# Three semaphores in turn for the indirect transfers of a routed layer, in place of two

## The chip, the cores and the metric

One Trainium2 chip, one NeuronCore of it. The metric is the device time of one execution in microseconds, as a median of several executions. PE is TensorE, DVE is VectorE, ACT is ScalarE, POOL is GpSimd, SP is SyncE.

## What is computed

A block of three layers on x of 4 x 1024 x 128 (f32): half a feed-forward layer, an attention layer, the same half feed-forward layer again, each on the layer norm of x and added to x.

```
x = x + 0.5 * ffn(layernorm(x))
x = x + attn(layernorm(x))       # 16 heads of 8, causal, with a slope bias
x = x + 0.5 * ffn(layernorm(x))

def ffn(x):                      # N = 4096 rows, D = 128, HID = 256
    gates = softmax(x @ router_w)            # 14 routed experts
    top_v, top_i = top_k(gates, 2)           # normed over the two
    routed = sum over the two chosen e: g_e * silu(rms(x)*rw_e @ W1_e) @ W2_e
    shared = sum over 2 shared experts, all rows
```

## The kernel before

The 4096 rows are 32 tiles of 128 rows, in two groups r = 0 and r = 1 of 16 tiles (GT). A feed-forward layer f (0 or 1) does its routed experts sparsely. DVE works out for each row its two experts and the place of each in a buffer `sorted_x[r]` in HBM, in which rows of one expert stand together. POOL then **scatters**: for each of the 16 tiles and each of the 2 choices one indirect transfer (L824) writes 128 rows of 512 bytes from SBUF to those places, so 32 transfers (MOVES) for a group. SP then loads `sorted_x` back in 23 pairs of tiles (L658, 128 KB each, `xld`), the first when all 32 scatters of the group have landed (L652). PE transposes a pair (L1819), multiplies it with the first weights of its experts (L1831), ACT does the silu, PE multiplies with the second weights (L1843), ACT brings the result to SBUF and stores it (`sorted_y`, L996). DVE copies the weights of the pair three ahead (L1373), each copy behind the product that frees the buffer. When all pairs of a group are stored, POOL **gathers**: 32 indirect transfers (L841) bring the rows back in order, and DVE multiplies them with the gates and adds them to x (`add_part`, L1182, eight parts for a group, each of which needs the transfers of its block of four tiles).

All 256 indirect transfers have one number n in a row, and a program order on POOL: scatter(0,0), scatter(0,1), gather(0,0), gather(0,1), then, in the second feed-forward layer, scatter(1,0), scatter(1,1), gather(1,0), gather(1,1), where the first number is f and the second r. What lies between them on POOL matters. The square roots for the attention's first norm (`norm(0)`, L745 to L747) stand behind the 18th gather of (0,0), waiting on DVE's statistics; a copy of the values (`values(0)`, L862) follows the 32nd; behind gather(0,1) POOL itself adds six of the eight parts of that group (`pool_adds`, L890 and L895), and only then does `norm(1)`, on whose result DVE waits in step 0 of the second group of heads of the first batch (`normed`, L1480; PE's next steps stand behind DVE). The other two parts of (0,1) are DVE's.

`keep_pace` holds back some scatters until PE has come to a given product, so that they don't all start at once.

A transfer waits on the semaphore that it will itself increment. These are the lines (L820 to L826 for a scatter, L839 to L844 for a gather):

```
n = MOVES * SCATTERS[GROUPS * f + r] + TOP_K * t + k
if n >= MOVE_SEMS:
    pool.wait_ge(s_moved[n % MOVE_SEMS], 16 * (n // MOVE_SEMS))
keep_pace(f, r, TOP_K * t + k)
nc.gpsimd.indirect_dma_start(...).then_inc(s_moved[n % MOVE_SEMS], 16)
```

and those who need the rows wait on all of the semaphores:

```
def moved(first, count):
    return [(s_moved[i], 16 * (sum(n % MOVE_SEMS == i for n in range(first + count))))
            for i in range(MOVE_SEMS) if any(n % MOVE_SEMS == i for n in range(first, first + count))]
```

At the end of the second feed-forward layer PE and ACT do 24 units of the shared experts (L1743, L950, L1762), 4 for each chunk of x left; gather(1,1) and its eight add_parts run beside them, four of the parts placed among the units (LATE_ADD_AT), four behind the last unit's sum (L1360). The result goes out in eight transfers (L703), each behind its block's adds.

Of the kernel before, what the change touches and what calls it, by code (L numbers as in the profile page):

```python
# [51 lines left out]
BLOCK = 4  # L52
BLOCKS = GT // BLOCK
MOVES = TOP_K * GT
MOVE_SEMS = 2
SCATTERS, GATHERS = (0, 1, 4, 5), (2, 3, 6, 7)

GH = 4
# [210 lines left out]
def build(nc, x, x_rows, w_qkv, w_proj, router_w, rms_w, w1, w2, rms_w_s, w1_s, w2_s, alibi, out):  # L269
    ctx = ExitStack()  # L270
    with ctx:
# [3 lines left out]
        def sem(name):  # L275
            return ctx.enter_context(nc.semaphore(name))
# [96 lines left out]
        def xh_tile(f, t):  # L373
            if f and GT <= t < GT + BT:
                return more_rows[:, t - GT, :]
            return xh[:, (t + GT) % TILES, :]
# [124 lines left out]

        s_moved = [sem(f"rows_moved{i}") for i in range(MOVE_SEMS)]
# [6 lines that stand above are left out]
# [199 lines left out]
        def _(pool):  # L708
# [90 lines left out]
            def keep_pace(f, r, move):  # L799

                o = ffn[f]
                if r:
                    pool.wait_ge(o.used, RING + SHARED_OF[f] + max(0, move - 8) // 2)
                elif f == 0 and move >= 12:
                    pool.wait_ge(o.used, RING + 2 + (move - 12) // 2)
                elif f and move < PACED:
                    pool.wait_ge(s_pv, 2 + (BATCH * UNITS - 1) * NS + SCATTER_STEP + move // 2)

            def scatter(f, r, first=0, end=MOVES):
# [6 lines left out]
                for t in range(GT):  # L816
                    for k in range(TOP_K):
                        if not first <= TOP_K * t + k < end:
                            continue
# [4 lines that stand above are left out]
                        nc.gpsimd.indirect_dma_start(  # L824
                            out=sorted_x[r], out_offset=bass.IndirectOffsetOnAxis(ap=pos[r][:, k, t:t + 1], axis=0),
                            in_=xh_tile(f, r * GT + t), in_offset=None).then_inc(s_moved[n % MOVE_SEMS], 16)  # L826

# [1262 lines left out]
```

## Time and profile before

| | |
|---|---|
| time, median of 3 runs | 1014.22 us (1011.94 to 1020.28) |
| profiled execution | 1006.91 us, span 1005.0 us |
| PE busy | 915.0 us, 91% |
| DVE, ACT, POOL busy | 659.6, 509.7, 386.5 us |
| POOL, instructions L824 (128 of them) | 129.8 us busy |
| DMA, mean share of the 16 engines in 40 slices | 0.97 at the start, 0.0 to 0.5 later |

The stages of the profiled execution, by POOL and PE: first feed-forward layer to about 222 us (scatter(0,0) 33 to 85, scatter(0,1) 91 to 142, gather(0,0) 149 to 212), attention from there to about 815, with gather(0,1) and pool_adds beside its first batch (215 to 305), second feed-forward layer from there (scatter(1,0) 790 to 835, scatter(1,1) 842 to 892, gather(1,0) 893 to 949, gather(1,1) 950 to 997). An indirect transfer's row in the timeline of POOL covers only the making of its descriptors; the transfer lands later.

### The profile page before, as it was taken

The page shows a single profiled execution, that of the slowest core. Times are in us where ns is not written, and L with a number is a line of the kernel's source. Part 1 is how long each engine was busy: PE and PEld are TensorE (multiplying, and loading weights), DVE is VectorE, ACT ScalarE, POOL GpSimd, SP SyncE. Part 2 cuts the span into 40 slices and gives each one's busy share as a digit, 9 for nine tenths or more (in the row PEclk, how much of TensorE's full clock was granted, in tenths as well). Part 3 has the DMA queues.
Part 4 walks back from the last instruction along what each step waited for, and adds up shares of the span by engine and source line. Part 5 has one row for each costly group of instructions (what it writes and reads, how often), then busy time and mean ns, then how long its engine had stood idle before and what let it go on. Part 6 is the DMA issues. An engine that isn't in the chain of part 4 may idle for free.

```text
span 1005.0 us, 19516 instructions
## 1 busy us (share of the span) xinstructions
PE 915.0 (91%) x6961; PEld 566.9 (56%) x6961; DVE 659.6 (66%) x1697; ACT 509.7 (51%) x826; POOL 386.5 (38%) x447
## 2 busy tenths in 40 slices
PE   5798979888897999999999999999999888969996
PEld 4576979762443444544444445444453347969864
DVE  5856325558695688797788877887868547324422
ACT  2333646440264566556655565665556654636531
POOL 4375655463671500002201005007500465564564
PEclk9979989995798999999999999999999997979998
DMA  9712545355102231400423102304000013546432
GB/s 300 229 48 76 175 125 166 98 165 139 47 4 51 70 87 28 97 4 17 117 51 74 26 1 86 87 13 96 4 3 1 27 48 103 171 120 163 129 84 66
DMA packets 84260, 85.36 MB, mean 85 GB/s; under 512 B 11732, under 2 KB 73444, under 8 KB 81700
## 3 DMA queue, kind: packets, MB, share of 16 engines
q1 hardware_dynamic: 50842, 55.08, 20.6%
q0 software_dynamic: 8192, 16.79, 6.0%
q10 hardware_dynamic: 25132, 12.26, 4.1%
q8 instruction: 56, 0.92, 0.4%
q14 instruction: 38, 0.31, 0.1%
HBM read 52.48 MB, written 37.45 MB: 89 GB/s over the span
## 4 chain that ended last, share of the span: by engine, by line
PE 53%; DMA 19%; DVE 11%; issue 6%; POOL 5%; ACT 2%; DVEq 2%; POOLq 1%; SPq 0%
PE banks L1939 10%; PE banks L1909 9%; DMA region_c<-sorted_y,pos 9%; PE banks L1922 9%; PE banks L1831 6%; PE banks L1843 6%; DMA region_b<-sorted_y,pos 4%; DVE nmax L1493 3%; DMA sorted_x<-region_b,pos 2%; POOL sorted_x L824 2%; PE banks L1925 2%; PE banks L1912 2%; PE banks L1819 2%; PE banks L1703 1%; DVE nmax_late_keys L1493 1%
## 5 line engine op out<-in xcount | busy, mean ns | idle before, releaser
L1077 ACT ACTIVATE work<-banks 128x1024 f32<-128x1024 f32 (+3 forms) x384 | 300.4, 812 | 234.3 <-PE banks L1925 185.5
L1493 DVE TENSOR_REDUCE nmax<-banks 128x1 f32<-128x512 f32 (+3 forms) x432 | 271.7, 665 | 49.8 <-PE banks L1909 23.5
L1909 PE MATMUL banks<-ks,qs 75*128 75x512 bf16 (+3 forms) x576 | 183.3, 347 | 10.4 <-DVE nmax L1493 5.8
L824 POOL DMA_INDIRECT sorted_x<-region_b,pos x112 | 113.3, 1012 | 142.0 <-DVEq L1315 76.7
L1939 PE MATMUL banks<-work,vaug 128*9 128x512 f32 (+3 forms) x1536 | 161.3, 492 | 0.0
L1922 PE MATMUL banks<-qs,ks 78*128 78x512 bf16 (+3 forms) x576 | 154.3, 330 | 4.1 <-ACT work L1077 3.2
L1373 DVE COPY region_c<-w 128x512 f32 x184 | 73.2, 439 | 110.5 <-PE banks L1843 101.1
L1493 DVE TENSOR_REDUCE nmax_late_keys<-banks 128x1 f32<-128x384 f32 (+3 forms) x176 | 109.4, 638 | 43.2 <-PE banks L1912 38.5
L1909 PEld LDWEIGHTS banks<-ks,qs 75*128 75x128 bf16 x576 | 55.9, 99 | 136.4 <-DVE nmax L1493 71.5
L1831 PE MATMUL banks<-xTp,region_c 128*128 128x128 f32 x736 | 102.4, 284 | 3.0 <-ACT xTp L977 2.5
L1925 PE MATMUL banks<-identb,maskb 128*128 128x128 bf16 x512 | 103.3, 221 | 0.0
L1912 PE MATMUL banks<-maskb,identb 128*128 128x128 bf16 x512 | 103.0, 226 | 0.0
L1843 PE MATMUL banks<-region_c,work 128*128 128x128 f32 x736 | 97.1, 275 | 0.0
L1831 PEld LDWEIGHTS banks<-xTp,region_c 128*128 128x128 f32 x736 | 94.0, 200 | 5.1 <-ACT xTp L977 4.5
L1843 PEld LDWEIGHTS banks<-region_c,work 128*128 128x128 f32 x736 | 89.8, 192 | 1.0 <-issue 1.0
L1762 PEld LDWEIGHTS banks<-w,work 128*128 128x128 f32 x512 | 68.7, 200 | 37.2 <-issue 24.9
L841 POOL DMA_INDIRECT region_c<-sorted_y,pos x64 | 60.8, 949 | 47.5 <-DMA region_c<-sorted_y,pos 41.5
L1922 PEld LDWEIGHTS banks<-qs,ks 78*128 78x128 bf16 x576 | 54.5, 99 | 43.2 <-ACT work L1077 11.4
L983 ACT ACTIVATE work<-banks 128x512 f32<-128x512 f32 x92 | 55.0, 598 | 46.9 <-PE banks L1831 46.5
L862 POOL TENSOR_TENSOR vaug<-region_b,one 128x128 f32<-128x128 f32 x32 | 13.0, 413 | 170.1 <-PE banks L1939 170.1
L1762 PE MATMUL banks<-w,work 128*128 128x128 f32 x512 | 71.5, 287 | 5.7 <-DVE xs L1360 4.0
L950 ACT ACTIVATE work<-banks 128x512 f32<-128x512 f32 x64 | 37.5, 597 | 71.4 <-PE banks L1743 69.7
(212 smaller groups left out, 1172.5 us busy)
## 6 DMA issues: line engine op xcount, KB each, us to landing
xld<-sorted_x SPq DMA_DIRECT2D x92, 128.0 KB
sorted_y<-ysb ACTq DMA_DIRECT2D x92, 128.0 KB
qs<-q_scr SPq DMA_DIRECT2D x36, 192.0 KB
ks<-k_scr SPq DMA_DIRECT2D x36, 192.0 KB
q_scr<-qp SPq DMA_DIRECT2D x15, 256.0 KB
region_c<-q_scr SPq DMA_DIRECT2D x12, 192.0 KB
region_c<-k_scr SPq DMA_DIRECT2D x12, 192.0 KB
k_scr<-kp SPq DMA_DIRECT2D x9, 256.0 KB
```

Source lines behind the costliest of these rows:

```text
L824: nc.gpsimd.indirect_dma_start(out=sorted_x[r], out_offset=bass.IndirectOffsetOnAxis(ap=pos[r][:, k, t:t + 1], axis=0), in_=xh_tile(f, r * ...
L1077: nc.scalar.activation(pT[s % 2][pair][:, :, 0:w], ps_s[pair][:, :, 0:w], ACT.Exp).then_inc(s_e, 1)
L1373: last = nc.vector.tensor_copy(w12c[q % WEIGHTS][:, a:a + 1, :], w12[:, bass.ds(es[a], 1), :])
L1493: nc.vector.tensor_reduce(dst, ps_in_turn[SLOT["bank", u * NB + n]][:, 0:len(pieces) * w].rearrange("p (h j) -> p h j", j=w), axis=AXX, op ...
L1762: last = mm(into[:, t * D:(t + 1) * D], uu[n % RING][:, t * P:(t + 1) * P], w2s[:, e, half, :], start=(m % NH == 0 and t == 0), stop=(m % ...
L1831: last = mm(ps_h[q % 2][:, at:at + P], w12c[q % WEIGHTS][:, a, half * P:(half + 1) * P], xTp[q % 2][:, a * P:(a + 1) * P], start=True, sto ...
L1843: last = mm(ps_y[q % 2][:, a * D:(a + 1) * D], uu[q % 2][:, at:at + P], w12c[q % WEIGHTS][:, a, HID + half * D:HID + (half + 1) * D], star ...
L1909: last = mm(dst, qs[g][0:PASS1_ROWS, h, it * P:(it + 1) * P], ks[g][0:PASS1_ROWS, h, j0:j0 + w], start=True, stop=not diagonal)
L1912: last = mm(dst[:, w - P:w], identb[:, :], maskb[:, :], start=False, stop=True)
L1922: last = mm(ps_s[pair][:, j, 0:w], ks[g][:, h, jt * P:(jt + 1) * P], qs[g][:, h, i0:i0 + w], start=True, stop=not diagonal)
L1925: last = mm(ps_s[pair][:, j, 0:P], maskb[:, :], identb[:, :], start=False, stop=True)
L1939: last = mm(ps_o[32 * h:32 * h + VW, i0 - HALF * ih:HALF], vaug[:, jt, g * GH + h, :], pT[s % 2][h // 2][:, h % 2, 0:w], start=(jt == 0), ...
```

## The change

One constant. Every transfer n then waits for transfer n - 3 in place of n - 2, three semaphores take turns, and `moved` gives three waits in place of two to SP (before the first load of a group), DVE (before each add_part) and POOL (before each part of pool_adds). The order of instructions is the same on every engine.

```diff
@@ -52,7 +52,7 @@
 BLOCK = 4
 BLOCKS = GT // BLOCK
 MOVES = TOP_K * GT
-MOVE_SEMS = 2
+MOVE_SEMS = 3
 SCATTERS, GATHERS = (0, 1, 4, 5), (2, 3, 6, 7)
```

## Rows read from the trace of the kernel before

**Rows 1.** Who waited for whom, PE: us in total, times, longest.

```profile
PE banks L1819 <- DMA xld<-sorted_x: 17.7, 5, 7.8
```

**Rows 2.** Timeline of PE: start, us, line, operation [idle before <- releaser].

```profile
145.84 1.12 PE L1819 MATMUL banks<-ident,xld 128*128 128x128 f32 x4 [5.72 <-DMA xld<-sorted_x]
...
190.88 1.97 PE L1965 MATMUL banks<-ident,region_a 128*128 128x128 f32 x8 [2.47 <-DVEq L1483]
...
308.91 1.09 PE L1992 MATMUL banks<-ident,oT 128*128 128x128 f32 x4 [5.70 <-DVE nmax_late_keys L1493]
...
838.72 1.09 PE L1819 MATMUL banks<-ident,xld 128*128 128x128 f32 x4 [2.76 <-DMA xld<-sorted_x]
...
895.69 1.31 PE L1819 MATMUL banks<-ident,xld 128*128 128x128 f32 x4 [7.77 <-DMA xld<-sorted_x]
```

**Rows 3.** Chain that ended last, in order of time: start, us, what.

```profile
824.25 2.22 DMA sorted_x<-region_b,pos
...
912.12 4.09 DMA xld<-sorted_x
...
950.11 2.48 DMA region_c<-sorted_y,pos
...
952.85 2.50 DMA region_c<-sorted_y,pos
```

**Rows 4.** Windows of POOL, L824 alone: us, busy (count), PEclk, DMA share, GB/s.

```profile
91.50:142.20 50.70, 31.94 (x32) 1.00 0.53 156
...
790.30:835.00 44.70, 31.77 (x32) 0.93 0.15 47
...
841.70:892.00 50.30, 32.41 (x32) 0.98 0.51 151
```

**Rows 5.** The same windows for L841, the gathers.

```profile
148.60:179.40 30.80, 18.16 (x18) 0.98 0.56 153
...
189.30:211.81 22.51, 15.35 (x14) 0.92 0.35 95
...
214.80:274.51 59.71, 30.33 (x32) 0.69 0.44 115
...
950.10:997.34 47.24, 30.43 (x32) 1.00 0.27 71
```

**Rows 6.** Timeline of POOL, columns as in Rows 2.

```profile
112.38 0.95 POOL L824 DMA_INDIRECT sorted_x<-region_b,pos  x1 [2.05 <-DMA sorted_x<-region_b,pos]
...
141.21 0.96 POOL L824 DMA_INDIRECT sorted_x<-region_b,pos  x1 [0.30 <-issue]
...
240.57 0.95 POOL L841 DMA_INDIRECT region_c<-sorted_y,pos  x1 [4.44 <-DMA region_c<-sorted_y,pos]
...
305.47 1.68 POOL L747 TENSOR_TENSOR rstd<-var_eps,minus_half 128x8 f32<-128x8 f32 x1
...
890.99 0.96 POOL L824 DMA_INDIRECT sorted_x<-region_b,pos  x1 [0.31 <-issue]
...
996.38 0.94 POOL L841 DMA_INDIRECT region_c<-sorted_y,pos  x1 [0.56 <-DMA region_c<-sorted_y,pos]
```

**Rows 7.** Timeline of DVE, columns as in Rows 2.

```profile
178.60 1.14 DVE L1182 SCALAR_TENSOR_TENSOR xs<-region_b,gates,xs 128x128 f32<-128x128 f32 x4 [3.08 <-DMA region_b<-sorted_y,pos]
...
297.72 0.25 DVE L1130 BATCH_NORM_AGGREGATE mva<-stats 128x2 f32<-128x6 f32 x2
...
307.30 0.86 DVE L1480 TENSOR_SCALAR region_a<-xs,mva,rstd 128x128 f32<-128x128 f32 x3 [5.54 <-POOLq L869]
...
996.48 0.69 DVE L1360 SCALAR_TENSOR_TENSOR xs<-banks,xs 128x512 f32<-128x512 f32 x1 [4.79 <-PE banks L1762]
...
999.88 2.35 DVE L1182 SCALAR_TENSOR_TENSOR xs<-region_c,gates,xs 128x128 f32<-128x128 f32 x8 [0.25 <-issue]
```

**Rows 8.** Windows of all engines: busy (count) of PE, PEld, DVE, ACT, POOL, PEclk, DMA, GB/s.

```profile
145.00:150.00 5.00, 4.12 (x19) 3.65 (x20) 0.00 (x0) 1.64 (x4) 1.04 (x2) 0.52 0.30 89
...
230.00:235.00 5.00, 4.42 (x15) 1.29 (x13) 4.53 (x7) 0.00 (x0) 0.95 (x1) 0.50 0.82 180
```

## The prediction

> **What bounds the kernel now.** The page's busy times come first: PE works for 91% of the span, so only the stretches in which PE stands still can give much. The second view is who waited for whom on PE: its largest sum is 17.7 us in five waits for `xld`, the load of a pair [rows 1]. The timeline of PE then places the waits. Two are large and stand at the same point of the two feed-forward layers, before the first pair of group 1: 5.72 us until 145.84 and 7.77 us until 895.69; a third, 2.76 us, ends at 838.72 before the first pair of the second layer [rows 2]. SP loads that pair only when all 32 scatters of its group have landed, and the timeline of POOL has the last of them issued at 141.21 and at 890.99 [rows 6], so these waits are the scatters'. Two more PE waits of that timeline lead to POOL as well. At 308.91 PE waited 5.70 us for DVE, and DVE had waited 5.54 us, until 307.30, for POOL's `norm(1)` [rows 7], whose root starts at 305.47 [rows 6], behind gather(0,1) and pool_adds. At 190.88 it waited 2.47 us for DVE's `normed` [rows 2]; DVE had stood 3.08 us until 178.60 for a gather of group (0,0) [rows 7], ahead of the statistics for that norm.
>
> **What a transfer costs.** In the chain, a scatter takes 2.22 us from its start on POOL to its landing and a gather 2.48, and the gather after next starts 0.26 us behind that landing (950.11 + 2.48, 952.85) [rows 3]. So two in flight allow one gather in (2.48 + 0.26)/2 = 1.37 us and one scatter in 1.24. POOL itself needs 0.96 us of its own and 0.30 us between two (the row at 141.21 [rows 6]): 1.26. In quiet stretches POOL is therefore already the bound for scatters, and gathers are 0.11 us above it. The gain lies in the transfers that land late. The windows tell how much POOL stood beyond its own work and its 0.30 us each: for scatter(0,1) 50.70 - 31.94 - 31 x 0.30 = 9.5 us, for scatter(1,0) 3.6, for scatter(1,1) 50.30 - 32.41 - 9.3 = 8.6 [rows 4]; for the gathers, 7.5 in the first 18 of (0,0), 3.3 in its last 14, 20.1 in (0,1), 7.5 in (1,1) [rows 5]. That is the most that any depth can give back.
>
> How much of it does a third transfer give? With three, a late one stops POOL only if it takes longer than 3 x 1.26 - 0.26 = 3.5 us; with two the limit is 2.26. I went through the 32 starts of each group in the timeline of POOL and took each landing as the start of the transfer after next less 0.26 us, wherever POOL had waited. In scatter(0,1) twelve took more than 2.6 us, but only two more than 3.5; the worst ended at 112.12, which POOL's 2.05 us wait before 112.38 shows [rows 6]. Replayed with start = the later of (end before + 0.30) and (landing of the third last + 0.26), the last scatter of (0,1) moves from 141.2 to 132.4 (8.8 of 9.5 us back), of (1,1) from 891.0 to 884.0 (7.0 of 8.6), and the last gather of (0,1) from 273.6 to 261.3 (12.3 of 20.1, since it has waits like the 4.44 us before 240.57 [rows 6], beside a DMA share of 0.82 [rows 8]). This holds if a landing takes no longer because a third is behind it. The other bound is that it gives nothing where the DMA engines are crowded.
>
> **The sum, part by part.** (1) Scatter(0,1): POOL starts it when it did, and 8.8 us less bring the pair to PE at about 137, ahead of the 140.1 at which PE is ready. The whole 5.72 us goes; below 5.72/9.5 = 60% recovered it goes in part. The stretch after this wait ran at a granted clock of 0.52, that is at the lower level of 1.2 GHz, with PE busy 4.12 of 5 us [rows 8]. At the upper level that work is up to 2 us shorter; the first pair is paced by ACT too, so I take 1.0. (2) Gather(0,0) starts some 5 us earlier with PE's earlier end of group 0 (its window began at 148.60 [rows 5]), and at 1.3 us a transfer its 16th lands near 166, while DVE now comes for it at 175.5 - 6.7 = 168.8. So DVE's 3.08 us go, and since from there to 190.88 PE is tied to DVE's statistics and norm, PE gains about 3.1. (3) The 5.70 us at 308.91: PE and DVE come there 5.7 + 1.0 + 3.1 = 9.8 us earlier, so POOL must be 9.8 + 5.7 = 15.5 earlier. `values(0)` and gather(0,1) start about 13 earlier (9.8 with PE, on whose time the last pair is stored, and 3.3 that the last 14 gathers of (0,0) lose today [rows 5]), and gather(0,1) gives 12.3 more, 25 in all. Even at a quarter of that last gain it is enough. The next latest is DVE's own statistics, ready at 297.97 [rows 7], after which `norm(1)` needs some 2 us, before DVE is there. So 5.7 go, and I estimate 0.9 of slow work behind the wait (the 1.09 us of that row [rows 2] at about half the clock, and the products after it). (4) Second layer: scatter(1,0) ends up to 3.6 us earlier, which would remove the 2.76 us at 838.72, but PE then only comes earlier to the wait at 895.69. That one is set by scatter(1,1), whose start hangs on DVE's placing of the rows and stays. So the two count together: 7.0 by the replay, 8.6 at most, 0 if the crowd decides. I take 6.5. (5) The tail: the chain that ended last goes through gather(1,1), but PE's last units end later than the gathers matter. DVE adds the last unit's sum at 996.48, having waited 4.79 us for PE, and reaches the last two parts at 999.88 with 0.25 us idle [rows 7]; the last gather, started at 996.38 [rows 6], lands at about 998.9. Its 7.5 us are worth nothing: PE and ACT hide them. Without that cover they would count nearly whole. Gather(1,0) likewise feeds only adds on DVE for which PE doesn't wait.
>
> What is added: a third wait on SP (4 times), on DVE (26) and on POOL (6). No row shows one such wait; the bound from above is the 0.30 us gap between two transfers, which holds a wait and an issue. Only the last few stand on the path: at most 1 us, probably 0.1. The dearer side is the crowd: gathers issued faster beside the key rows' stores and loads before attention, and beside `xld`. Nearest is the 20.1 us that gather(0,1) itself lost to such a crowd [rows 5]; spread the other way over a few loads I take 1.0 us lost, from 0 to 5. Sum: 5.7 + 1.0 + 3.1 + 5.7 + 0.9 + 6.5 - 1.1 = 21.8. The profiled execution would go from 1006.9 to 985, and the median, 1014.2 (7 above the profiled one), to 1014.2 - 21.8, or 992.4. I forecast 993.
>
> **Rivals.** (A) The late landings are a share of bandwidth, not a delay: a third transfer then only queues behind the other two, and in crowded stretches each lands later by as much as it was issued earlier. For it speaks the stretch from 230 to 245 (DMA share 0.82 [rows 8]); against it, that scatter(0,1) and (1,1) have a share of 0.53 and 0.51 [rows 4] and gathers (0,1) do half of their waiting at about 0.8. Then the waits of (1) and (4) stay, and what is left is (3) in part, through some 3.5 us of quiet gathers, and perhaps 1 of (2): 4.5 us, 1010. The Trainium skill (DMA: Bandwidth & Descriptors, Queues, rings and completion order) says that each DMA engine takes the queues that have work in turn, a packet at a time. By that rule a queue that is never empty gains nothing from a third transfer, so wherever two in flight keep it filled the rule gives rival A's time. The windows' mean shares near a half agree with it less than with a queue that runs empty while POOL waits.
>
> (B) Half the landings' waits come back. Then (1) is 4.8 with its clock cost left, (2) 1.5, (3) 5.7 (its margin is large), (4) 4, less 1.1: 15, and 999.
>
> (C) The tail counts: if the last gather did bound the end, as the chain draws it, 7.5 more: 985.
>
> (D) Slower: the pair loop's loads. PE takes a pair in 2.0 us, and its load is issued two pairs ahead, so a load may take about 3.7 us until PE stands; today one of 4.09 us stands in the chain, with PE behind it [rows 3]. If denser indirect transfers made that the usual load, each of the 92 pairs would lose 4.09 - 3.7 = 0.4 us: 37 us against the 22 of the sum, so it decides from a mean load of about 3.9 us on, where the loss passes the gain. At 4.0 us it ends at 1014.2 + 28 - 22, or 1020. Against it, the bytes are the same and the indirect traffic in those stretches grows only from one transfer in 1.6 us to one in 1.3.
>
> That the change does nothing is possible only if `keep_pace`, not the landing, holds the scatters; then DMA would not be named before the waits of the scatters [rows 6].
>
> **How the numbers follow.** Chances: forecast 0.68, B 0.13, A 0.10, C 0.04, D 0.05. The forecast's own spread is 986 to 999 (part 4 between 5 and 8.6, crowd 0 to 5, medians that differ by some us). The range takes in B with its spread: 985 to 1005. A measurement here can tell about 1%, 10 us, from no change. Faster by more than that: the forecast, C and most of B, 0.82; within 1%: A, some of B and D, 0.14; slower: 0.04.
>
> **What the profile after would show.** POOL's window of scatter(0,1) near 42 us and of scatter(1,1) near 43; no PE wait before the first pair of group 1 of the first layer, and one of under 4 us in the second layer; no DVE wait for a gather near 168; no DVE wait for `norm(1)`; gather(1,1) done well before PE's last unit, whose distance to the end stays about 8 us. The forecast fails if landings grow with the third transfer (then the windows keep their length), or if a wait moves to the loads (L1819 then gets many small waits), or if another of DVE's or SP's waits is found just behind the one removed at 308.91.

## The result and the profile after

The changed kernel takes 983.66 us in the median (981.14 to 987.73, 4 runs) against 1013.08 for the kernel before on the same chip (1010.29 to 1020.28): a ratio of 0.970, 95% interval 0.966 to 0.973. The change makes it 3.0% faster. The profiled executions are 1006.91 and 982.65 us, 24.3 apart; the medians are 29.4 apart.

The page of the kernel after, its busy times and the slices of PE:

```profile
span 980.7 us, 19519 instructions
...
PE 908.4 (93%) x6961; PEld 561.9 (57%) x6961; DVE 658.8 (67%) x1697; ACT 510.0 (52%) x826; POOL 389.6 (40%) x447
...
PE   5798999988999999999999999999999888989996
```

The work is the same (DVE and ACT within 1 us, POOL 3 us more); what went is PE's standing still, and 7 us of PE's own busy time, by its clock work at the lower level (the mean granted clock is 0.950 before and 0.962 after). The waits of [rows 1], again five, come to 3.7 us, the longest 2.2:

```profile
PE banks L1819 <- DMA xld<-sorted_x: 3.7, 5, 2.2
...
PE banks L1965 <- DVEq L1483: 2.2, 1, 2.2
```

The timeline of PE after, at the places of [rows 2]:

```profile
138.98 0.60 PE L1819 MATMUL banks<-ident,xld 128*128 128x128 f32 x4
...
180.61 1.09 PE L1965 MATMUL banks<-ident,region_a 128*128 128x128 f32 x8 [2.22 <-DVEq L1483]
...
292.81 0.63 PE L1992 MATMUL banks<-ident,oT 128*128 128x128 f32 x4
...
819.78 1.09 PE L1819 MATMUL banks<-ident,xld 128*128 128x128 f32 x4 [0.69 <-DVE xs L1360]
...
873.06 0.44 PE L1819 MATMUL banks<-ident,xld 128*128 128x128 f32 x2 [2.19 <-DMA xld<-sorted_x]
```

Read the first number of each row against its fellow: 10.3 us earlier at L1965 (190.88 before), 16.1 at L1992 (308.91), 18.9 at the second layer's first pair (838.72). The waits of 5.72 and 5.70 us are gone and that of 7.77 is 2.19. The third row also tells the clock: the same four products of L1992 took 1.09 us behind the wait and take 0.63 us now.

POOL's windows after, with the columns of [rows 4] (time, busy and count, granted clock, DMA share, GB/s). They are, in turn, scatter(0,1), gather(0,0), gather(0,1), scatter(1,1) and gather(1,1); the second holds two instructions of the norms besides:

```profile
90.84:133.60 42.76, 32.32 (x32) 1.00 0.57 169
142.46:200.30 57.84, 37.24 (x34) 1.00 0.51 139
203.37:255.60 52.23, 30.31 (x32) 0.67 0.51 131
824.88:869.20 44.32, 33.07 (x32) 1.00 0.54 161
925.60:966.10 40.50, 30.28 (x32) 1.00 0.31 83
```

The two scatters last 42.8 and 44.3 us in place of 50.7 and 50.3, gather(0,1) 52.2 in place of 59.7. Beyond POOL's own work and 0.30 us for each, scatter(0,1) now stands 1.2 us, scatter(1,1) 1.9 and gather(1,1) 0.9, by sums over their starts. Gather(0,0) stands 11.3, nearly all of it for DVE's statistics ahead of `norm(0)` and only 0.7 for landings. Gather(0,1) still stands 12.7, nearly all of it at rows like these on POOL, which answer to the 4.44 us before 240.57 [rows 6]:

```profile
227.29 0.94 POOL L841 DMA_INDIRECT region_c<-sorted_y,pos  x1 [3.07 <-DMA region_c<-sorted_y,pos]
229.65 0.94 POOL L841 DMA_INDIRECT region_c<-sorted_y,pos  x1 [1.41 <-DMA region_c<-sorted_y,pos]
232.48 0.94 POOL L841 DMA_INDIRECT region_c<-sorted_y,pos  x1 [1.89 <-DMA region_c<-sorted_y,pos]
235.91 0.94 POOL L841 DMA_INDIRECT region_c<-sorted_y,pos  x1 [2.48 <-DMA region_c<-sorted_y,pos]
237.15 0.96 POOL L841 DMA_INDIRECT region_c<-sorted_y,pos  x1 [0.31 <-issue]
```

There the DMA engines are still crowded. The window of all engines from 228 to 233 has a share of 0.82, as [rows 8] had:

```profile
228.00:233.00 5.00, 4.26 (x13) 0.92 (x12) 4.43 (x8) 0.00 (x0) 1.70 (x3) 0.50 0.82 182
```

### The profile page after: what moved, and what is told of

The parts are those of the page before. It is cut to its first block, busy times and chain, and to the rows that moved or that the text cites. A ratio compares the mean times of both kernels' runs of the same rounds, so it can differ in the third digit from the quotient of the medians.

```text
span 980.7 us, 19519 instructions
## 1 busy us (share of the span) xinstructions
PE 908.4 (93%) x6961; PEld 561.9 (57%) x6961; DVE 658.8 (67%) x1697; ACT 510.0 (52%) x826; POOL 389.6 (40%) x447
## 4 chain that ended last, share of the span: by engine, by line
PE 67%; DVE 17%; DMA 5%; issue 4%; DVEq 3%; ACT 3%; POOL 2%; POOLq 0%; ACTq 0%; SPq 0%
PE banks L1909 11%; PE banks L1939 11%; PE banks L1922 10%; PE banks L1831 7%; PE banks L1843 7%; DVE nmax L1493 5%; PE banks L1762 4%; PE banks L1743 4%; DVE nmax_late_keys L1493 2%; PE banks L1912 2%; PE banks L1925 2%; PE banks L1703 2%; PE banks L1819 2%; ACT work L1077 2%; POOL region_b L841 2%
## 5 line engine op out<-in xcount | busy, mean ns | idle before, releaser
L824 POOL DMA_INDIRECT sorted_x<-region_b,pos x112 | 114.5, 1023 | 127.8 <-DVEq L1315 76.9
L1831 PE MATMUL banks<-xTp,region_c 128*128 128x128 f32 x736 | 99.3, 279 | 3.1 <-issue 1.7
L1831 PEld LDWEIGHTS banks<-xTp,region_c 128*128 128x128 f32 x736 | 91.1, 195 | 4.3 <-ACT xTp L977 2.3
L1762 PEld LDWEIGHTS banks<-w,work 128*128 128x128 f32 x512 | 68.7, 200 | 37.3 <-issue 24.9
L841 POOL DMA_INDIRECT region_c<-sorted_y,pos x64 | 60.6, 947 | 40.9 <-issue 16.7
L1762 PE MATMUL banks<-w,work 128*128 128x128 f32 x512 | 71.5, 287 | 5.7 <-DVE xs L1360 4.1
```

The source lines that it names most:

```text
L824: nc.gpsimd.indirect_dma_start(out=sorted_x[r], out_offset=bass.IndirectOffsetOnAxis(ap=pos[r][:, k, t:t + 1], axis=0), in_=xh_tile(f, r * ...
L841: nc.gpsimd.indirect_dma_start(out=got_rows(f, r, k, t), out_offset=None, in_=sorted_y[r], in_offset=bass.IndirectOffsetOnAxis(ap=pos[r][: ...
L1762: last = mm(into[:, t * D:(t + 1) * D], uu[n % RING][:, t * P:(t + 1) * P], w2s[:, e, half, :], start=(m % NH == 0 and t == 0), stop=(m % ...
L1831: last = mm(ps_h[q % 2][:, at:at + P], w12c[q % WEIGHTS][:, a, half * P:(half + 1) * P], xTp[q % 2][:, a * P:(a + 1) * P], start=True, sto ...
```

## Experiments

The experiments were made on four different chips, called the second to the fifth here, with the kernel before beside them on each; the first is that of the result (the record doesn't tell whether it is one of the four). The second chip differs from the others, and that turned out to matter. Ratios are to the kernel before on the same chip. The edits are shown shortened.

**On the second chip: both kernels again, depth without a gain, and a fourth transfer.** e1 and e2 are the two kernels unchanged. e3 has three semaphores and waits for the third last and the second last, so that two are under way:

```
-MOVE_SEMS = 2
+MOVE_SEMS = 3
-pool.wait_ge(s_moved[n % MOVE_SEMS], 16 * (n // MOVE_SEMS))
+for d in (3, 2):
+    pool.wait_ge(s_moved[(n - d) % MOVE_SEMS], 16 * ((n - d) // MOVE_SEMS + 1))
```

e4 is the changed kernel with `MOVE_SEMS = 4`.

> The kernel before, unchanged, to see how its executions spread. Theory L (landings): the 7 us by which the median of before lies above its profiled execution is time that late landings cost in other executions, at the same PE waits. Then a new profile shows the waits for xld and for norm(1) larger or smaller by as much as its span differs from 1005, and the times spread over 8 us or more, with a median near 1013. Rival M (median by chance): the times gather near 1007 to 1010, and the spread lies in stretches without indirect transfers (clock, attention).

> The changed kernel, unchanged. Theory L: its times spread less than those of before (under 5 us), since a third transfer takes in late landings; the ratio stays near 0.970. Rival M: spread as wide as before, ratio nearer to 0.976, which is what the two profiles give.

> Three semaphores in turn, but each transfer also waits for the second last, so only two are under way. Every step of the prediction gives no change: 1013, within 3 us, and the PE waits of 5 to 8 us before the first pair of group 1 stay. If the semaphores themselves or the third waits on SP, DVE and POOL cost anything, it shows here alone: at most 1 us slower.

> Four semaphores, four transfers under way. By the 3.5 us limit only a few landings were later than three in flight take in (1.2 us of POOL's standing left in scatter(0,1), 1.9 in scatter(1,1)), so 0 to 2 us faster than with three: ratio 0.968 to 0.971 to the kernel before. If more depth made the loads of pairs late (rival D), PE's waits at L1819 grow in number and it ends slower than with three, 985 or more.

Measured: e1 1077.99 us (ratio 1.002), e2 1182.49 (1.105, 1.095 to 1.114), e3 1058.23 (0.990, 0.980 to 0.999), e4 1182.79 (1.106). Everything is slower on this chip, and the change loses 10% there. The loss is not a wait for a landing. The timelines of e2 on DVE, PE and ACT show it in the second layer, during gather(1,1):

```profile
1100.57 1.05 PE L1762 MATMUL banks<-w,work 128*128 128x128 f32 x8
...
1133.98 0.69 DVE L1360 SCALAR_TENSOR_TENSOR xs<-banks,xs 128x512 f32<-128x512 f32 x1 [38.83 <-remote]
...
1134.73 2.07 PE L1762 MATMUL banks<-w,work 128*128 128x128 f32 x8 [32.25 <-DVE xs L1360]
...
1129.04 0.60 ACT L950 ACTIVATE work<-banks 128x512 f32<-128x512 f32 x1 [19.69 <-remote]
```

DVE stands for 38.83 us until the products of L1762 are signalled. The last of them ended at 1101.6, so the signal is some 32 us late, and no record of PE ends anywhere near the end of that wait ("remote" is the view's word for a releaser that it doesn't find). The stall ends with POOL's rows:

```profile
1126.84 0.94 POOL L841 DMA_INDIRECT region_c<-sorted_y,pos  x1 [0.30 <-issue]
1128.08 0.94 POOL L841 DMA_INDIRECT region_c<-sorted_y,pos  x1 [0.30 <-issue]
```

which are the last of a train of gathers at 0.30 us between two. ACT goes on at 1129.04 and DVE five us later. Gather(1,0), from 1001 to 1040, has the same picture (17.84 us on PE, until 1043.12). In e1 such idles come where POOL happens to issue almost without a gap (19.63 and 21.35 us on ACT and DVE near 75, beside scatter(0,0)). In no run did they come in the attention stretch, where POOL moves no rows. Idle times of over 1.2 us whose releaser the view gives as "remote" or "issue" add up to 27, 74 and 129 us on PE, ACT and DVE in e1, to 76, 154 and 147 in e2 and to 7, 25 and 40 in e3, whose two waits keep POOL off its floor; in the first chip's kernel before there are none and in the kernel after 1.7 us on PE. Some "issue" idles are ordinary waits. "Remote" alone, it is 68 us on ACT and 93 on DVE in e1, 142 and 138 in e2, and 2.6 and 2.3 in e3, and no run on another chip has any. In e2 and e4, in each such idle of over 5 us POOL starts nearly all of its transfers 1.24 to 1.3 us apart. So on this chip a signal of PE reaches ACT and DVE late in the stretches in which POOL issues indirect transfers back to back, and the change makes it do so for longer. The link is one of time and of four kernels: no run on this chip varies POOL's pitch alone, and why this chip and no other shows it stays open. For the same reason e3 doesn't tell by itself what a third semaphore costs without depth.

**On the third chip: the changed kernel again, and the third transfer for one kind alone, with a second wait.** e5 is the changed kernel. In e6 the gathers, in e7 the scatters wait for the second last too, as e3 does. e8 lets three be under way, but each eighth transfer waits for all before it:

```
+if n % 8 == 0:
+    for d in (2, 1):
+        pool.wait_ge(s_moved[(n - d) % MOVE_SEMS], 16 * ((n - d) // MOVE_SEMS + 1))
```

> The changed kernel again. On the chip of e1 to e4 it took 1182 us against 1081 of the kernel before, and in both PE's signals came to ACT and DVE up to 39 us late, only in stretches in which POOL issues indirect transfers back to back at its floor of 1.26 us; on the chip of the result (983.66 against 1013.08) no such delay shows. Theory C (a property of the chip): on this run's chip either both kernels are as in the result (ratio about 0.97, no waits on late signals over 1.2 us), or both have late signals and the changed kernel the more (ratio 1.05 to 1.12). Rival V (by chance, varies from run to run on any chip): times in between, the ratio anywhere.

> Three under way for the 128 scatters, two for the 128 gathers (a gather waits for the second last too). By the prediction's steps scatters carry (1) and (4), that is 5.7 + 1.0 + 6.5 = 13 us; on a chip like that of the result: ratio 0.985 to 0.989. On a chip with late signals: slower than before by 2 to 5%, since the scatters then run at the floor.

> Three under way for the gathers, two for the scatters. By the prediction's steps gathers carry (2) and (3): 3.1 + 5.7 + 0.9 = 10 us, ratio 0.989 to 0.992 on a chip like that of the result, if (2) and (3) don't need the earlier start that (1) gives. On a chip with late signals: slower, with the long stalls beside the gathers of the second layer (38.8 and 19 us in e2).

> Three under way, but each eighth transfer waits until all before it have landed: one transfer in (7 x 1.26 + 2.74)/8 = 1.45 us at best. If late signals are let through whenever POOL waits, no signal can be later than about 10 us, and on such a chip this is faster than the changed kernel by 30 us or more; if POOL's waiting has nothing to do with it, they stay as in e2. On a chip like that of the result it costs up to 6 us per group of 32, of which PE sees those at the two scatters and at gather(0,1): 0 to 12 us slower than the changed kernel.

Measured: e5 983.50 us (0.970, 0.965 to 0.975), e6 1024.19 (1.011), e7 1014.85 (1.000), e8 1007.55 (0.995). e5 repeats the result, without one late signal. e6 and e7 missed: each should have kept its part of the gain, and neither gained. Their POOL rows say why they don't count as a test of depth. In e6, in a quiet stretch of gather(0,1):

```profile
249.74 0.94 POOL L844 DMA_INDIRECT region_c<-sorted_y,pos  x1 [1.10 <-DMA region_c<-sorted_y,pos]
250.98 0.95 POOL L844 DMA_INDIRECT region_c<-sorted_y,pos  x1 [0.30 <-issue]
252.97 0.94 POOL L844 DMA_INDIRECT region_c<-sorted_y,pos  x1 [1.03 <-DMA region_c<-sorted_y,pos]
254.22 0.94 POOL L844 DMA_INDIRECT region_c<-sorted_y,pos  x1 [0.30 <-issue]
```

Two gathers take 3.23 us (249.74 to 252.97). The kernel before, also with two under way, takes 2.74 for them (950.11 to 952.85 [rows 3]). Over all of gather(0,1) it is 2.04 us for each transfer in place of 1.89, and norm(1) makes PE wait 12.05 us. In e7 it is the scatters: scatter(0,1) takes 58.5 us in place of 50.7. So the two waits in a row cost some 0.5 us for each two gathers beyond the depth itself, and whatever limits the depth by them measures them too. e8's gain is small for the same reason, or since each eighth transfer gives back what seven won; it doesn't tell which.

**On the fourth chip: the third transfer for one kind alone, each kind with semaphores of its own.** Every transfer waits for one semaphore, as in the kernels compared:

```
-MOVE_SEMS = 3
-s_moved = [sem(...) for i in range(MOVE_SEMS)]
+MOVE_SEMS = (3, 2)        # e9: scatters, gathers; e10: (2, 3)
+s_moved = [[sem(...) for i in range(MOVE_SEMS[kind])] for kind in range(2)]
...
+if r == 0:
+    for s, count in moved(0, 0, MOVES * GROUPS * (f + 1)):
+        pool.wait_ge(s, count)
```

The last lines stand ahead of a layer's first gather, and let it wait for all scatters; the second layer's first scatter waits for all gathers before it in the same way. e11 is e4 again. e12 is the changed kernel with a tiny write on POOL and its drain ahead of each transfer:

```
+nc.gpsimd.memset(pause[:, :], 0.0)
+pool.drain()
 nc.gpsimd.indirect_dma_start(...)
```

> Scatters and gathers have semaphores of their own (three for the scatters, two for the gathers), so that each transfer still waits for one semaphore alone, and nothing but the depth differs from the kernel before; at each change of kind the first transfer waits for all of the other kind. Theory of the prediction (its parts add up, each from its own group of transfers): the scatters alone carry the terms (1) and (4), 6.7 and 7.0 us, so the time is about 13.7 us below that of the kernel before beside it (ratio 0.986 to 0.988); TensorE's first routed pair starts without a wait, scatter(1,1) ends with an excess under 3 us, and the waits behind gather(0,0) and gather(0,1) come back (DVE 3 us, norm(1) 6 us). Rival: the parts don't stand alone, one depth is worth nothing without the other (as the two kernels with a second wait read, 1.011 and 1.000): ratio 0.995 or more.

> The mirror image: two semaphores for the scatters, three for the gathers. Theory of the prediction: the gathers alone carry the terms (2) and (3), 3.1 and 6.2 us, so about 9.3 us below the kernel before (ratio 0.990 to 0.992); the wait of the first routed pair of layer 1 (5.7 us) and of layer 2 (7.8 us) stay, the norm(1) wait goes. This one and its mirror image together then give 23 us, what the profiled executions show of the whole change. Rival: the second wait was not what slowed the two earlier kernels, and this one gives 0.997 or more.

> Four transfers may be under way. On a chip where the changed kernel gives 0.970: the scatters and the second layer's gathers already run at POOL's own pitch with three, and only gather(0,0) and gather(0,1) still wait (excess 13.2 and 12.7 us), of which nothing that TensorE waits for is left but 2.2 us of the load of keys and 2.2 us at the first pair of layer 2. So 0 to 4 us below three under way: ratio 0.966 to 0.971. Rival (crowding): a fourth transfer in the queue lengthens the loads beside it, and the ratio is 0.973 or more. On a chip like the one of the first job the ratio is again above 1.09.

> Three under way, with a tiny write on POOL and its drain ahead of each transfer, so that POOL is never back to back at its floor. Theory of the late signals (TensorE's semaphore signals are late only while POOL issues indirect transfers at its floor): on a chip that shows late signals the pause takes them away, and the kernel comes from 1.105 to 0.99 or less. On a chip that doesn't show them, the pause only costs its own time: each transfer some 0.1 to 0.4 us more, 32 of them 3 to 13 us; after's slack behind scatter(0,1) is 6 us and behind scatter(1,1) none, so the ratio is 0.972 to 0.985. Rival (the late signals come from the number in flight): on such a chip the pause changes nothing, 1.09 or more.

Measured: e9 1005.47 us (0.992, 0.989 to 0.994), e10 996.49 (0.986, 0.982 to 0.989), e11 984.74 (0.973, 0.969 to 0.976), e12 1419.89 (1.405). The kernel before beside them has 1012.48.

Three scatters alone give 7.0 us and three gathers alone 16.0. Their sum is the 23 us that was expected, but the shares are the other way round (13.7 and 9.3), and the whole change gives 29 to 30: some 6 us come only when both are deeper. These two also say what the second wait alone costs: e6 takes 18.7 us more than e9 and e7 18.4 more than e10, at equal depths (on two chips with the same time for the kernel before). Gather(1,1), two under way in both, takes 56.9 us in e6 and 47.0 in e9. Both kinds with a second wait would then take some 1050 us, an estimate from these differences. e3 took 1058 on the second chip, so little else slowed it there. The timeline of PE in e9 shows where the scatters' gain goes; its lines stand 8 further down, so that L2000 is L1992 and L1770 is L1762:

```profile
185.59 1.09 PE L1973 MATMUL banks<-ident,region_a 128*128 128x128 f32 x8 [2.47 <-DVEq L1491]
...
308.81 1.09 PE L2000 MATMUL banks<-ident,oT 128*128 128x128 f32 x4 [9.36 <-DVE nmax_late_keys L1501]
...
954.80 1.93 PE L1770 MATMUL banks<-w,work 128*128 128x128 f32 x8 [3.86 <-DVE xs L1368]
```

PE is 5.3 us early at the first row. At the second it is where it was (308.81, before 308.91), since gather(0,1) ends where it did and the wait for norm(1) has grown from 5.70 to 9.36. The third is a wait that no profile of the kernel before or after shows so long: DVE stands for gather(1,0) until 951.50 and frees PE's bank late, so much of the 7.8 us of the second layer is given back too:

```profile
951.50 2.38 DVE L1190 SCALAR_TENSOR_TENSOR xs<-region_a,gates,xs 128x128 f32<-128x128 f32 x8 [9.21 <-DMA region_a<-sorted_y,pos]
```

From the second layer's first pair to the last L1743, e9 is 1.7 us shorter than the kernel before (152.3 and 154.0), where the changed kernel is 5.4 shorter. Another part of what this execution lost is no wait for rows: its last step of attention is 4.4 us longer than in the kernel before, with PE at a granted clock of 0.59 and no long wait ahead:

```profile
800.00:810.00 10.00, 10.00 (x40) 0.59 0.15 48
```

The same step has such a stretch in some executions of the kernels compared (e5 and e15, 0.70, some 2 us) and not in others.

On top of the gathers, the scatters' gain stays: 0.970 against 0.986 is 13 to 16 us across chips, where 13.2 were forecast for the parts (1) and (4). In e10, the norm's wait is gone, both waits for scatters stand:

```profile
145.63 1.12 PE L1827 MATMUL banks<-ident,xld 128*128 128x128 f32 x4 [6.35 <-DMA xld<-sorted_x]
...
302.46 0.63 PE L2000 MATMUL banks<-ident,oT 128*128 128x128 f32 x4
...
889.15 1.29 PE L1827 MATMUL banks<-ident,xld 128*128 128x128 f32 x4 [8.52 <-DMA xld<-sorted_x]
```

A fourth transfer changes nothing that can be measured; gather(0,1) stands 9.1 us in place of 12.7, and PE doesn't wait for it. The loads of pairs aren't crowded by it either: PE's longest wait for one is 0.5 us.

e12 could not test the late signals, since this chip has none, but it missed by 400 us, and its rows on POOL tell why:

```profile
111.91 0.96 POOL L827 DMA_INDIRECT sorted_x<-region_b,pos  x1 [1.92 <-issue]
112.87 0.11 POOL L825 MEMSET pause<- 128x1 f32 x1
114.91 0.96 POOL L827 DMA_INDIRECT sorted_x<-region_b,pos  x1 [1.92 <-issue]
```

The write takes 0.11 us, but with it and its drain (the run doesn't tell them apart) the transfer starts 1.92 us later, not 0.30. A transfer costs 3.0 us and more. POOL's eight groups together last 477 us longer than in the kernel after, and the time is 436 us longer. That also says what a slower POOL costs: little of it is hidden.

**On the fifth chip: more profiles.** e13 to e15 are the kernel before, e16 the changed one, one execution each.

> The kernel before again, for its profile alone. Theory: the 7 us by which its median lies above its profiled execution lie in the waits for landings, those of the gathers above all (with three gathers under way the executions spread over 5 to 7 us, with two over 8 to 16), so a profiled execution whose time is some us above 1006.9 shows a longer wait of norm(1) or of the first pairs (TensorE's 5.7, 5.7 and 7.8 us) and a later end of gather(0,1) or scatter(1,1), and the same busy times. Rival: the 7 us are spread over the span (TensorE's clock or its busy time), and a slower execution has the same waits.

> As the one before it: a further profiled execution of the same kernel. Waits for landings longer by what the time is longer (theory), or the same waits and a longer busy time or lower clock (rival).

> As the two before it: a further profiled execution of the same kernel.

> The changed kernel again, for its profile beside those of the kernel before on the same chip. Theory: its waits for landings are short in any execution, so its landmarks lie within some 2 us of the first profile's, and its distance to the profiled executions of the kernel before is 24 us where theirs is near 1007 and up to 30 us where theirs is near 1013.

Measured: 1015.65, 1015.57 and 1018.72 us for the kernel before, 986.45 for the changed one, a distance of 29.1 to 32.3 in place of the first pair's 24.3. PE at its marks, in us (the last column is the row of L1743 with x2 ahead of the last L1762):

```
                    L1965   L1992   (its wait)   L1717   L1819   L1743    span
first chip, before  190.88  308.91     5.70      783.84  838.72   992.74  1005.0
e13                 191.91  315.77    11.17      792.02  847.42  1001.40  1013.6
e14                 191.41  313.14     6.08      792.88  848.43  1001.42  1013.6
e15                 190.24  311.77     9.46      790.13  845.62  1001.80  1017.0
first chip, after   180.61  292.81     none      766.41  819.78   968.40   980.7
e16                 181.19  297.77     none      771.61  824.77   972.26   984.5
```

e16 missed its expectation: its marks lie up to 5.2 us from the first profile's, not 2, so a single execution of the changed kernel isn't exact either. Of the two theories for e13 to e15, neither holds alone. In e14, 8.7 us slower than the first profile, the wait for norm(1) is only 0.4 us longer; 3.7 us are lost between L1965 and the end of that wait and 4.8 behind it, where the lower clock lasts longer, as the rival had it. In e13 and e15 the wait is 5.5 and 3.8 us longer.

Take e16 as the partner of e13 to e15. At L1965 the distance is 9.1 to 10.7 us, as in the first pair. At L1992 it is 14.0 to 18.0 (first pair 16.1), so that the longer waits for norm(1) don't lengthen it in the mean, and at L1717 18.5 to 21.3 (17.4). From L1992 to L1717 the changed kernel takes 473.6 and 473.8 us, the kernel before 474.9, 476.3, 479.7 and 478.4, with the same small waits. The windows of PE in e14 show what that is:

```profile
307.00:313.00 6.00, 0.06 (x1) 0.65 0.17 45
313.00:318.00 5.00, 4.86 (x26) 0.50 0.77 157
318.00:323.00 5.00, 5.00 (x23) 0.50 0.21 41
323.00:328.00 5.00, 5.00 (x26) 0.50 0.00 0
328.00:333.00 5.00, 5.00 (x29) 0.87 0.01 3
```

Behind the wait, which ends at 313.14, PE has the lower level of its clock (1.2 GHz, a granted clock of 0.50) for some 16 us, with PE busy throughout. On the first chip the wait ends at 308.91 and the upper level is back about 314:

```profile
308.00:313.00 5.00, 4.09 (x22) 0.50 0.76 169
313.00:318.00 5.00, 4.94 (x41) 0.94 0.30 61
```

In e15 part of the longer way lies elsewhere (the clock is 0.73 and 0.58 from 515 to 525, with no long wait ahead of it). From L1717 to the last L1743 come 8.7, 7.9 and 11.0 us more (first pair 6.9), of which 2.3 in e15 are the slow attention step named above, so that the last L1743 is 29.1 to 29.5 us apart. And in e15 alone the end is bounded by the gathers, for 3 us: DVE waits 3.20 us where [rows 7] had 0.25.

```profile
1011.88 2.35 DVE L1182 SCALAR_TENSOR_TENSOR xs<-region_c,gates,xs 128x128 f32<-128x128 f32 x8 [3.20 <-DMA region_c<-sorted_y,pos]
```

## Why the prediction was right, and where it failed

The mechanism was right: late landings, not the mean, held POOL, and PE stood for them at three places. The time fell 1.3 us below the range, 8.7 below the 992.4 of the sum. Of this, 1.1 is the median of the kernel before (1013.1 with one more run), 2.5 the sum itself and 5.2 the step from profiled executions to medians. By the prediction's steps:

**(1) and (2), before attention**, 9.8 us less what the crowd takes: PE is 10.3 us earlier at L1965. The first pair of group 1 starts at 138.98, without a wait, where 137 and 140.1 had been named, and the stretch behind it has its full clock (0.60 us for four products of L1819, before 1.12). Right. But e9 shows that (1) had a condition which was not said: 5.3 us gained there alone are lost again at norm(1), 9.36 in place of 5.70.

**(3), the norm**, 5.7 + 0.9 = 6.6: 5.8 us by L1992 and 1.3 by L1717, where a late norm had left PE at the lower clock. Right in the profiled pair. The replay's 12.3 us for gather(0,1) were 7.2, since the crowd from 208 to 236 did not change; the margin of which the prediction spoke covered that. The next latest is DVE's statistics, as named: POOL now waits 1.57 us for them.

**(4), the second layer**, 6.5: 1.5 at its first pair and 5.4 behind it, 6.9 together. Right in the profiled pair. Of 7.77 us 2.19 stay.

**(5), the tail**, 0: the last L1743 to the end takes 12.3 us before and after. Right for that execution; e15 shows that in others it counts up to 3 us. Rival C was thus wrong in the profile and in part true of one of the three others.

**What is added and the crowd**, 1.1: nothing of it shows. The loads did not get slower (rival D): the five waits for `xld` sum to 3.7 us. Rival A is out by POOL's windows, and half the waits (B) as well, except in the one crowded stretch, which behaves nearly as A has it: POOL stood 15.4 us for landings there before (rows from 223 to 246) and stands 12.5 after. The Trainium skill (DMA: Bandwidth & Descriptors, Queues, rings and completion order) says that each DMA engine takes the queues that have work in turn, a packet at a time. What the prediction worked out from it, that a queue that is never empty gains nothing from a third transfer, fits that stretch, at a share of 0.82, though no view shows whether POOL's queue was ever empty there; the windows at shares near a half are decided without it.

**The step that failed** is the last one of the sum: "the median, 1014.2 (7 above the profiled one), to 1014.2 - 21.8". The sum itself was 21.8 against 24.3 between the profiled executions. But it was taken from one profile at the fast end of its kernel's times (1006.9, in runs of 1010 to 1020), and the 7 us were assumed to be outside of what the change touches. The runs show the contrary in large part: the medians lie 6.2 us above the profiled execution for the kernel before and 1.0 for the changed one. The profiled execution, 1006.9, is faster than each of the 42 others of the kernel before outside the second chip. So three terms, read from its rows, were mis-sized for an ordinary execution. Against e16, the slow work behind norm(1) in (3) is worth 2.4, 5.9 and 4.5 us from L1992 to L1717, where 0.9 was taken and 1.3 measured in the first pair; (4) is worth 8.7, 7.9 and 11.0, where 6.5 was taken; the tail (5) 0, 0 and 3, where 0 was. Over the first pair that is 2.9, 2.3 and 1.0 us in the mean, 6.2 together, where 5.2 are missing. With three profiles and one partner these shares are rough.

What makes one execution slower than another is only in part the landings. In the 19 executions of the kernel before on the third chip the time goes with the mean granted clock (0.952 in the fastest, 1007.9 us, and 0.937 in the slowest, 1020.6; correlation -0.85). A wait lowers the clock behind it, but e14 has nearly the first profile's wait and three times the slow stretch, and the slow attention step of e5, e9 and e15 has no wait ahead at all. What sets the length of such stretches stays open. Nor is it shown that a third transfer narrows the spread: on the fourth chip the times lie within 8 us for the kernel before (15 runs), 5 for e10 (5 runs) and 16 for e9 (11 runs), though the first and the last both have two gathers under way.

What the prediction could not have had from its profile is the second chip, where the same change costs 10%.

## What to carry to other kernels

Size a wait for landings by more than one execution: the one profiled may be the luckiest, and a late wait costs its length and then the lower clock behind it, which varies more than the wait does. Where a queue of transfers is kept at a fixed depth, one semaphore a transfer and a third in turn is worth a try as soon as single landings take more than twice the issuing engine's pitch, but deepen all of its users together, since in e9 most of what the scatters gained was given back at the gathers. Limit a depth by the number of semaphores and not by a second wait, and measure on several chips before you keep it.

## What the runs showed of the hardware

- On one chip of the four of the experiments, PE's signals reach ACT and DVE late while POOL issues indirect transfers 0.30 us apart (e2: DVE stands 38.8 us, 32 of them after the product had ended). The kernel before takes 1078 to 1081 us there and 1012 to 1013 in three other jobs.
- On POOL, an indirect transfer of 128 rows takes 0.95 us and 0.30 to the next. Two waits ahead of each, with two under way, make two gathers take 3.23 us in place of 2.74 (e6); with a write of 0.11 us and its drain ahead, the 0.30 us become 1.92 (e12).
- After a wait of 6 us PE's clock stayed at its lower level for 5 us in one execution (the first profile) and 16 in another (e14), with PE busy throughout; after one of 11 us (e13) it was 6.
